# Attention prologue of a fused attention and MoE kernel: weight units placed between the projections of the first four slots

## The reference, cut to what matters

```python
x = x + xattn(_layernorm(x), ctx_2048, ...)
x = x + ffn(_layernorm(x), ...)          # router, 8 experts top 2, and a shared MLP
# xattn
ln_out = _ln(hidden_states, ln_w, ln_b)
q  = _ln(fp8_linear(ln_out, wq))     # 16 heads of 128
k  = _ln(fp8_linear(ln_out, wk))     # 8 heads
v  = fp8_linear(ln_out, wv)
core = gqa(q, k, v)
qx = _ln(fp8_linear(ln_out, wqx))
kx, vx = split(ctx @ w_kv_x.T)       # kx = _ln(kx)
xout = gqa(qx, kx, vx)
return fp8(concat(core, xout) / proj_smooth) @ wproj.T * scales
```

## Time and profile before

| | |
|---|---|
| median of 3 runs | 1063.23 us (1062.16 to 1063.65) |
| profiled execution | 1064.14 us, span of its instructions 1062.4 us |
| busy, share of the span | PE 92%, PE weight load 65%, DVE 76%, ACT 69%, POOL 39% |
| granted PE clock, mean | 0.967 of full speed |

### The profile page before, as it was taken

The page is one execution under the profiler, slowest core; times in us unless marked ns, Lnnn a source line. Parts: engine busy times, 40 slices in busy tenths (PEclk is TensorE's granted clock), DMA queues, the critical chain, the costliest instruction groups (busy, mean ns, idle before and its releaser), DMA issues. The chain is left out here.

```text
span 1062.4 us, 23698 instructions
## 1 busy us (share of the span) xinstructions
PE 976.8 (92%) x7206; PEld 695.6 (65%) x7207; DVE 805.8 (76%) x1710; ACT 735.3 (69%) x1344; POOL 416.7 (39%) x630
## 2 busy tenths in 40 slices
PE   4586999999999999999999999699999789999994
PEld 2464777777777777777777777575556546666663
DVE  5577999999999999999999999889566634444442
ACT  5876888888888888888888887365455335445452
POOL 4224644455445454445544545103630013323322
PEclk9798999999999999999999999859999989999998
DMA  9910301010010000100001010133542165222222
GB/s 261 251 60 16 85 22 39 20 37 22 20 39 20 27 32 20 39 20 34 27 21 41 21 41 21 60 119 116 175 167 83 57 184 105 25 30 25 25 30 25
DMA packets 32819, 65.43 MB, mean 62 GB/s; under 512 B 3712, under 2 KB 20736, under 8 KB 32512
## 3 DMA queue, kind: packets, MB, share of 16 engines
q1 hardware_dynamic: 23312, 50.20, 14.4%
q0 software_dynamic: 9456, 14.59, 7.8%
HBM read 53.42 MB, written 16.59 MB: 66 GB/s over the span
## 5 line engine op out<-in xcount | busy, mean ns | idle before, releaser
L592 POOL TENSOR_TENSOR root<-vareps,neghalf 128x4 f32<-128x4 f32 (+1 forms) x128 | 173.6, 1356 | 10.0
L585 POOL TENSOR_TENSOR var<-ssq,unit 128x4 f32<-128x4 f32 (+1 forms) x128 | 54.2, 424 | 298.7 <-DVE ssq L452 298.7
L323 PE MATMUL b_pj<-w_hi,xq 128*128 128x512 f16 x384 | 148.0, 385 | 0.5 <-ACT raw L406 0.5
L323 PE MATMUL b_pj<-w_lo,xq 128*128 128x512 f16 x384 | 147.1, 383 | 0.0
L396 ACT ACTIVATE sq<-b_pj 128x512 f32<-128x512 f32 x192 | 114.1, 594 | 44.4 <-PE b_pj L323 43.2
L1477 POOL DMA_INDIRECT out<-xg x39 | 60.6, 1553 | 208.6 <-ACT xg L1578 179.6
L452 DVE TENSOR_REDUCE ssq<-sq 128x4 f32<-128x512 f32 x192 | 130.1, 678 | 13.2 <-ACT sq L396 13.1
L463 DVE TENSOR_TENSOR nrm<-raw,rstd 128x512 f32<-128x512 f32 x192 | 128.3, 668 | 5.1 <-POOL rstd L596 4.4
L339 PE MATMUL b_tr<-ident,nrm 128*128 128x128 f32 x768 | 116.9, 275 | 12.8 <-DVE nrm L463 9.6
L349 PEld LDWEIGHTS b_sc<-kT,qT 128*128 128x128 f32 x1024 | 123.1, 192 | 7.0 <-ACT qT L422 0.3
L349 PE MATMUL b_sc<-kT,qT 128*128 128x64 f32 x1024 | 121.4, 272 | 0.0
(11 more groups left out here) (282 smaller groups left out, 2323.7 us busy)
## 6 DMA issues: line engine op xcount, KB each, us to landing
nst<-in_ffw SPq DMA_DIRECT2D x30, 512.0 KB, 3.1
wload<-in_ffw SPq DMA_DIRECT2D x30, 512.0 KB
xbuf<-zero SPq DMA_DIRECT2D x39, 129.0 KB, 4.0
xg<-xbuf SPq DMA_DIRECT2D x9, 516.0 KB
x_sb<-in_x SPq DMA_DIRECT2D x4, 512.0 KB, 20.4
wproj<-in_ctxT SPq DMA_DIRECT2D x1, 2048.0 KB, 9.3
xq<-in_w_all SPq DMA_DIRECT2D x4, 512.0 KB, 14.6
wproj<-in_wprojT POOLq DMA_DIRECT2D x4, 512.0 KB, 7.7
```

Source lines behind the costliest of these rows:

```text
L323: last = pe.matmul(o, x, w[:, k, at:at + BANK], start=(k == 0 and n_ == 0), stop=(k == KT - 1 and n_ == len(terms) - 1))
L592: pool.tensor_tensor(root[:, r % 2, c, :], vareps[:, r % 2, c, :], neghalf[:, 0:1].unsqueeze(2).to_broadcast(shape), ALU.pow).then_inc(s[" ...
```

## The change

1. **Units in the slots.** `run_slots` gets a fourth argument, `behind`: a label on a step of the list, and for (slot, label) a function that runs right behind that step. `between` is now empty except for `early` on DVE and POOL's `token_rstd` and `output_weights`. Units 0, 1, 2 stand ahead of the first token work, unit 3 behind its transpose; units 4 to 11 stand in pairs between the projections of slot -3, 12 to 19 in slot -2, 20 to 27 in slot -1 (20 and 21 already behind its first transposes, with the context scale ahead of them on DVE and, on PE, the scale's matmul behind them), 28 to 31 in slot 0.
2. **Tile 0.** Its quantized parts alternate with units; part 3 comes in slot -3.
3. **Sums of squares** at the end of slots -3 and -2 on ACT, **statistics** at the end of slots -3, -2 and -1 on DVE, with POOL's `token_rstd` ahead of slots -2, -1 and 0.
4. **The context's rest**: ACT's high halves in slot 0 behind `raw 2`, DVE's low halves in slot 0 behind `squares 2`, POOL's loads of the output weights ahead of slot 1.
5. ACT starts with a copy of four elements, which loads its function table; `b_sum` is in bank `b_pt`; SP issues the token tiles ahead of the float32 blocks.
6. **MoE tail.** In the slot of tile 36, where tile 38 is the last, `first(38)` stands behind `second(36)` and `product_T(37)`, with the same move on ACT and DVE.

```diff
-            def run_slots(eng, steps, between):
+            def run_slots(eng, steps, between, behind):
                 def slot(i, r):
-                    for ahead, step in steps:
+                    for ahead, step, *label in steps:
...
+                        if label and isinstance(i, int):
+                            behind.get((4 * i + r, label[0]), lambda: None)()
...
+                for c in range(1, 4):
+                    sp.dma_start(x_sb[:, 4 * c:4 * c + 4, :], x_t[:, 4 * c:4 * c + 4, :]).then_inc(s[f"x_in{c}"], 16)
                 for g in (2, 3):
                     for m in (0, 3):
...
-                for c in range(1, 4):
-                    sp.dma_start(x_sb[:, 4 * c:4 * c + 4, :], x_t[:, 4 * c:4 * c + 4, :]).then_inc(s[f"x_in{c}"], 16)
...
-                weights(0, (0,))
+                weights(0, 0, 1, 2)
                 pe_token_T(pe, 0, 0)
-                weights(0, (1, 2, 3))
+                weights(0, 3)
...
-                ], {-2: second_weights, -1: third_weights, 0: last_weights})
+                ], {}, {
+                    (-3, "project 0"): lambda: weights(0, 4, 5), (-3, "project 1"): lambda: weights(0, 6, 7),
+                    (-3, "project 2"): lambda: weights(1, 0, 1), (-3, "project 3"): lambda: weights(1, 2, 3),
+                    (-2, "project 0"): lambda: weights(1, 4, 5), (-2, "project 1"): lambda: weights(1, 6, 7),
+                    (-2, "project 2"): lambda: weights(2, 0, 1), (-2, "project 3"): lambda: weights(2, 2, 3),
+                    (-1, "first transposes"): third_weights, (-1, "project 0"): lambda: weights(2, 6, 7),
+                    (-1, "project 1"): lambda: weights(3, 0, 1), (-1, "project 2"): lambda: weights(3, 2, 3),
+                    (0, "first transposes"): lambda: weights(3, 4, 5), (0, "project 0"): lambda: weights(3, 6, 7),
+                })
...
                 act.wait_ge(s["cols_in"], 16)
+                act.activation(sqsum[:, 0:4], col[:, 0:4], ACT.Copy)
...
-                ], {-2: second_weights, -1: third_weights, 0: last_weights, 1: context_rest})
+                ], {}, {
...
+                    (-3, "raw 2"): last_part, (-3, "raw 3"): lambda: high(1, 2, 3), (-3, "tokens"): context_squares,
...
+                    (0, "raw 2"): context_high,
+                })
...
+                    (-3, "tokens"): lambda: statistics(1),
...
+                    (0, "squares 2"): lambda: context_low(2, 1, NT),
...
-                        if exists(t + 2):
+                        if exists(t + 2) and exists(t + 3):
                             first(t + 2, n % 2, es[n + 2])
-                        if exists(t + 3):
                             gather_T(t + 3, (n + 1) % 2, (n + 3) % TURN)
                         second(t, n % 2, es[n])
                         if exists(t + 1):
                             product_T(t + 1, (n + 1) % 2)
+                        if exists(t + 2) and not exists(t + 3):
+                            first(t + 2, n % 2, es[n + 2])
```

More of the change, by code:

```diff
@@ L612, in weights @@
                             pe.wait_ge(s[name], count)
[L613 to L622, removed]
+                        u = 8 * g + n
+                        after(pe, "wlo_done", u - len(b_w) + 1)
+                        for hd in range(HC):
+                            last = pe.matmul(b_w[u % len(b_w)][:, hd * D:(hd + 1) * D], w[:, hd, k * P:(k + 1) * P],
+                                             mat[:, :], start=True, stop=True)
+                        last.then_inc(s["wc_done"], 1)
                 def third_weights():
-                    weights(2, (0, 1))
+                    weights(2, 4, 5)
                     pe.wait_ge(s["csum_done"], 1)
                     pe.matmul(b_sum[:, 4:6], ones[:, :], csum[:, :], start=True, stop=True).then_inc(s["ctot_done"], 1)
-                    weights(2, (2, 3))
-                def last_weights():
-                    weights(3, range(4))
                 pe.wait_ge(s["sum_ones"], 1)
@@ L852, in _ @@
                 dve_token_norm(dve, 0, 0)
-                for part in range(4):
-                    dve_quantize(dve, 0, part)
-                low(0, range(4))
+                low(0, 0, 1, 2)
+                dve_quantize(dve, 0, 0)
+                low(0, 3)
+                dve_quantize(dve, 0, 1)
+                dve_quantize(dve, 0, 2)
                 run_slots(dve, [
-                    (PREP, dve_token_norm),
+                    (PREP, dve_token_norm, "token norm"),
                     (1, dve_max),
@@ L873, in _ @@
                     (-1, dve_round),
-                    (PREP, dve_quantize),
-                ], {-2: second_weights, -1: third_weights, 0: last_weights, 1: context_rest, 2: last_statistics,
-                    4 * (NT - 1): early})
+                    (PREP, dve_quantize, "tokens"),
+                ], {4 * (NT - 1): early}, {
+                    (-3, "squares 0"): lambda: low(0, 4, 5), (-3, "squares 1"): lambda: low(0, 6, 7),
+                    (-3, "squares 2"): lambda: low(1, 0, 1), (-3, "norm 0"): last_part,
+                    (-3, "tokens"): lambda: statistics(1),
+                    (-2, "squares 0"): lambda: low(1, 4, 5), (-2, "squares 1"): lambda: low(1, 6, 7),
+                    (-2, "squares 2"): lambda: low(2, 0, 1), (-2, "norm 0"): lambda: low(2, 2, 3),
+                    (-2, "tokens"): lambda: statistics(2),
+                    (-1, "token norm"): third_weights, (-1, "squares 0"): lambda: low(2, 6, 7),
+                    (-1, "squares 1"): lambda: low(3, 0, 1), (-1, "squares 2"): lambda: low(3, 2, 3),
+                    (-1, "tokens"): lambda: statistics(3),
+                    (0, "token norm"): lambda: low(3, 4, 5), (0, "squares 0"): lambda: low(3, 6, 7),
+                    (0, "squares 2"): lambda: context_low(2, 1, NT),
+                })
                 dve.wait_ge(s["st3_done"], NT)
@@ L1599, in slot @@
                         high_T(t + 1, 1 - n)
+                    if exists(t + 2) and not exists(t + 3):
+                        gate(t + 2, n)
+                        split(t + 2, n)
                 slots(act, slot)
@@ L1644, in slot @@
                         low_T(t + 1, 1 - n)
+                    if exists(t + 2) and not exists(t + 3):
+                        product(t + 2, n)
+                        split(t + 2, n)
                 slots(dve, slot)
```

143 lines of the change are left out of this document (67 added, 76 removed).

## The result

The changed kernel takes **1057.18 us** (median of 6 runs, 1056.21 to 1058.71), the kernel before, run beside it, 1062.7 us. The ratio is 0.995, 95% interval 0.9939 to 0.9962: faster by 5.5 us. The forecast was 4.8 us off 1063.2, so 1058.4, in 1054.5 to 1062.5.

A forecast was written before the change was run, and what follows sets the result against it. The prologue was taken as bound by ACT's work and waits up to slot -1, then the scale's chain and DVE. Full clock 5.4 + 0.9 + 0.1 = 6.4, half 3.7; taken 4.8 off 1063.2, so 1058.4 us, range 1054.5 to 1062.5.

The forecast's parts named there:

- Slot -3 to the scale: Prologue: first projection at 12.9, squares' sum 46.1 or 48.8, scale 48.5 or 51.1, slot -1's projection 5.7 or 3.4 earlier.
- ACT's walk: Slots -3 and -2, stepped through in order: added waits of 0.3 and 2.3 us at full clock, 1.1 and 4.2 at half.
- Half clock in slots -3 and -2: If PE runs at half clock throughout these two slots, the whole gain is 3.7 us.
- two sums: Total gain 6.4 us at full clock or 3.7 at half clock in slots -3 and -2; 4.8 was taken.
- From there to the one at 73.96 it took 17.2. ... 17.4 ...: the same.: Slot -1's context projection to slot 0's: 17.4 us from DVE's work plus PE's and ACT's hand-overs, against 17.2 before.
- Slot 0 and the stall: Slot 0's projection to token norm 17.8 us, DVE waiting 4.4; PE's stall moves to slot 1's first transposes, 7 to 9.
- Statistics: Leaving slot 0 offsets the work coming in there; in slot 2, 0.9 of the 1.6 us is gained.
- The tail: MoE tail: additions are chained 4.55 us apart, so the move gains at most 0.1 us and loses 0.
- B: Rival: PE stays at 1.2 GHz through slots -1 and 0, costing 4.9 us; 1.2 us slower, 1064.4; chance 0.07.
- C: Rival: ACT's waits shrink by 2.6 us and PE runs slots 1 and 2 without waits; gain 9, 1054.2; chance 0.12.
- D: Rival: each of 14 places with a pair of units costs a full pass beyond the walk; slower, 1065.4; chance 0.08.
- E: Rival: units move but ACT's total stays and the wait goes elsewhere; gain under 3, mostly under 2.1; chance 0.13.

The follow-up runs named there:

- experiment 6: Changed kernel plus 16 unread matmuls of 512 columns on PE in the wait for the context's scale: 1055.78 us, ratio to before 0.9942.
- experiment 8: Changed kernel with the context's rest in three pieces, 16 unread matmuls in the scale's wait and 24 behind slot 1's scores: 1051.10 us, ratio 0.9906.
- experiment 12: Changed kernel with unread matmuls in both waits (16 and 32), the context's rest in one piece: 1057.67 us, ratio to before 0.993.
- experiment 10: Kernel before plus unread matmuls in its two long PE waits, 28 ahead of units 18 and 19, 36 in slot 1: 1064.28 us, ratio 1.0016.
- experiment 3: Changed kernel with the statistics of x put back ahead of slots 0, 1 and 2: 1058.82 us, ratio to before 0.9968.
- tail only: Kernel before with only the MoE tail's move: 1062.28 us, ratio to before 1.0002.
- experiment 5: Changed kernel with the context's rest back ahead of slot 1, as in the kernel before: 1056.70 us, ratio to before 0.996.
- experiment 4: Changed kernel with the context's rest in three pieces on ACT and DVE: 1056.68 us, ratio to before 0.9952.

## Why the prediction was right, and where its sum was not

- **Slot -3 to the scale: right.** First projection 12.9 forecast, 12.87; squares' sum 46.1 at full clock, 45.94; scale 48.5, 48.1 to 48.2; slot -1's projection 51.0, 50.90. The gain there was forecast as 5.7 at full clock and is 5.8. An agreement within 0.2 us is luck: over nine traces with the new order the squares' sum lies between 45.94 and 47.41, 46.5 in the mean, and over four of the old one between 46.91 and 47.45. The table load is shown apart (1.28 forecast, 1.3 measured). Why ACT's walk held is argued from its agreement at four moments. No run took the units' places alone: with 1.3 for the table load and 1.3 for the statistics, they are left with 2.9 of 5.5, or 1.7 of 4.3, by subtraction.
- **Half clock in slots -3 and -2: only in part.** In slot -3 only the first matmuls are slow; from 15.8 on a matmul of 512 columns takes 0.38, and the stretch from 12 to 25 us is granted 1.00 with PE busy 9.6 of 13. In slot -2 PE does run at the lower level, from 31.82 to about 36.4, behind its wait of 4.39 us. The prediction had named that wait (low halves which ACT makes late), but not its clock. By the walk the half clock cost little there: ACT waits 1.34 and 0.84 us for transposes in this slot, 2.2 in all, where the walk had 2.3 at full clock and 4.2 at half. The Trainium skill, "TensorE: Matmul & The Clock Gate", section "A second HAM failure mode: psum-queue depth-cycling", had pointed to a clock that keeps falling back where groups cycle through PSUM banks. From 12 to 25 us, three banks in turn, the trace doesn't show it; the lower level comes behind a single long wait. Over 13 to 45 us, the stretch by which the prediction meant to decide between its two sums, the grant is 0.89, the same as in the kernel before.
- **The term that was mis-sized: "From there to the one at 73.96 it took 17.2. ... 17.4 ...: the same."** It took 19.66. The parts that the term names make 14.6, and the other 2.8 of "PE's and ACT's hand-overs" have no row. PE's clock was not in the term. The wait for the scale, which I had as 2.4 us of small operations and 2.5 of first halves, leaves PE idle for 4.30 us, and PE then does a projection and two float32 units at the lower level (0.52 granted, 1.2 GHz). Experiments 6, 8 and 12 give the stretch without that: 16.84, 16.84 and 16.83. So the term should have been 16.8 and a price of the clock, 2.8 in the profiled execution and 1.4 to 2.9 over six, and the gain at slot 0 is 3.4, not 5.5. The kernel before paid for its wait of 6.54 us too (half clock until 52.6; experiment 10 takes 1.8 off A), but ahead of its projection at 56.74, so its 17.2 held nothing of that. In the change the same kind of price lies behind the projection at 50.90.
- **Slot 0 and the stall: right.** DVE's wait 4.4 forecast, 4.34; PE's stall 7 to 9, 7.18; slot 0's projection to token norm 17.8, 17.7.
- **Statistics: right in the sum.** From slot 0's projection to slot 2's scores it took 25.97 before and 26.03 with the change, so the statistics that left slot 0 only pay for what came in, as forecast; in slot 2 (scores to scores) 10.18 became 9.01, 1.2 where 0.9 was forecast. It was the expectation of experiment 3 that counted too much: the 1.6 at the token norm don't reach PE.
- **The tail: right**, 0.0 to 0.1.
- **The sum.** The forecast of 4.8 stood between two sums, 6.4 and 3.7, told apart by the clock in slots -3 and -2. (Three of its steps are 0.1 to 0.2 us off by their own terms: the first projection comes to 12.8, 51.1 and 2.5 make 53.6, and 17.8 is 0.2 above 17.6, so the sums are 6.3 and 3.3.) The measured 5.5 lies between them for another reason: mostly full clock there, half behind the scale. That the forecast came so near is therefore partly luck, since a guess for one loss covered another. By the moments of the profiled pair, 3.4 at slot 0's projection and 1.1 behind it make 4.5; with the second trace of each order, slot 3's scores start at 110.11 and 111.06 (tail only) in the old one and at 105.60 and 105.20 in the new, 5.2 apart in the mean, which is the median's difference within 0.3. The second comparison of the same two kernels gave 4.3.
- **The rivals.** B, the clock eats it, named the right place, slot -1, and the right cause, but with 4.9 us and on top of half clock before; the price is 1.4 to 2.9. C needed ACT's waits to go, and in slot -2 they stayed at 2.2. D's places cost nothing measurable beyond the walk: eight of the 14 stand ahead of the squares' sum, which came at 45.94, and the stretch with the next ones takes 16.8 us at full clock, less than the forecast's 17.4. E, gain under 3, falls with 5.8 at slot -1 and with both medians. That the context's rest was moved is indeed without effect (experiment 5), as the working said.

## What to carry to other kernels

When a walk through engines gives each wait its length, add to every long wait of TensorE what the work behind it costs at half clock; here the 4.3 us wait cost 1.4 to 2.9 more, and in these traces shortening a wait paid fully only when the clock was held. Unread matmuls in such a wait are cheap, if they can start at once, in a bank that is free, and end before the operand arrives: 16 and 24 of them with the context in three pieces were worth more than the change itself (6.2 against 4.3 us on the same chip, 5.5 on the first). And a move whose engine has slack, such as the tail or the context's rest, should be costed by what bounds the end there, and then often be left alone.

## What the runs showed of the hardware that was not expected

The clock came back sooner or later behind the same wait, and how soon PE began to work does not tell when: with the transposes at 87.38 it was full at 90.85, at 85.56 (experiment 4) at 90.73, at 86.14 (experiment 6) already at 89.43, and at 89.35 (experiment 5) at 92.78. With them at 83.10 behind fillers it had never fallen. Fillers themselves start at whichever level PE has: 16 took 5.30 us in experiment 6 and 3.61 in experiment 8, in the same place, so the length of a filler can't be set exactly. Ahead of the scale's matmul, just in front of them, PE had been idle for 2.01 us in experiment 6 and for 0.38 in experiment 8. And with PE busy for all of 51 to 57 us the grant was 0.52, the 1.2 GHz level: a PE that shows as busy all the time may be waiting for its clock.
